# Layer 0 of a sparse graph-attention stack runs inside the load stage, a step for each loaded tile

## The reference

```python
def _L0_gnn_ref(inputs, adj, W, a):
    Wh = inputs @ W
    e = (Wh @ a[:F_out, 0])[:, None] + (Wh @ a[F_out:, 0])[None, :]
    e = jnp.where(e > 0, e, ALPHA * e)
    scores = jnp.where(adj > 0, e, NEG_BIG)
    attention = jax.nn.softmax(scores, axis=1)
    return jax.nn.elu(attention @ Wh)
...
x = _layernorm(x + _L0_gnn_ref(x, adj, L0_gnn_W, L0_gnn_a), axis=-1)
x = _layernorm(x + _L1_gnn_ref(...), axis=-1)   # slope 0.01, a bias, no elu
x = _layernorm(x + _L2_gnn_ref(...), axis=-1)   # as layer 0
x = _layernorm(x + _L3_gnn_ref(...), axis=-1)   # slope 0.01, elu
```

## Time and profile before

| | us |
|---|---|
| median of 3 runs | 621.22 (620.89 to 625.52) |
| the profiled execution, its own time | 624.31 |
| its span, first to last instruction | 622.4 |
| DVE, ACT, PE and POOL busy in the span | 408.7, 364.4, 361.5, 330.4 |
| indirect gathers on POOL | 340, 330.2 busy |
| adjacency transfers | 32 of 2048 KB |

### The profile page before, as it was taken

How to read it: one execution, slowest core, us unless ns; L and a number is a source line. 1 busy time by engine, 2 the same in 40 slices (tenths; PEclk the granted TensorE clock), 3 DMA queues, 4 the chain that set the end, 5 groups by cost and what they waited for, 6 DMA issues and landing times.

```text
span 622.4 us, 11074 instructions
## 1 busy us (share of the span) xinstructions
PE 361.5 (58%) x3546; PEld 322.1 (52%) x3558; DVE 408.7 (66%) x1830; ACT 364.4 (59%) x797; POOL 330.4 (53%) x344
## 2 busy tenths in 40 slices
PE   2365422323332589885278777527887752787663
PEld 1254311322222589784278667427877642786662
DVE  2897869799979628896235768623575862357576
ACT  3575775766674268883076667307666740676563
POOL 0000574156555700017777777767777777777760
PEclk9999999999999989996599989659988975999896
DMA  7998999999993200002222222222222222222220
GB/s 264 416 400 311 365 368 403 420 405 401 413 408 110 25 1 10 19 21 49 29 27 28 37 47 47 45 29 30 28 37 46 45 46 32 29 37 36 44 45 22
DMA packets 22084, 86.74 MB, mean 139 GB/s; under 512 B 6851, under 2 KB 12102, under 8 KB 17798
## 3 DMA queue, kind: packets, MB, share of 16 engines
q1 hardware_dynamic: 10102, 73.39, 29.4%
q0 software_dynamic: 10880, 11.51, 13.4%
q10 hardware_dynamic: 1040, 1.08, 0.5%
HBM read 80.58 MB, written 5.37 MB: 138 GB/s over the span
## 4 chain that ended last, share of the span: by engine, by line
POOL 32%; DMA 18%; DVE 15%; issue 13%; ACT 10%; PE 8%; POOLq 0%; ACTq 0%; DVEq 0%
POOL xg L392 32%; DMA arena<-in_adj_t 16%; ACT arena L679 6%; PE bank L590 3%; PE bank L564 2%; DVE key L1093 2%; DVE arena L1066 1%; DMA xg<-table,index 1%; DVE stats L1118 1%; ACT arena L705 1%; PE bank L453 1%; DVE found L868 1%; DMA table<-wh 1%; DVE mean_var L1121 1%; DVE key L1115 1%
## 5 line engine op out<-in xcount | busy, mean ns | idle before, releaser
L392 POOL DMA_INDIRECT xg<-table,index x340 | 330.2, 971 | 274.7 <-issue 98.7
L705 ACT ACTIVATE arena<-bank,sloped_own 128x256 f32<-128x256 f32 (+3 forms) x144 | 76.8, 536 | 142.3 <-PE bank L564 141.6
L1066 DVE CUSTOM_DVE_ANT_0 arena<-bank,arena 128x256 f32<-128x256 f32 (+3 forms) x144 | 71.3, 499 | 130.9 <-ACT arena L705 130.7
L679 ACT ACTIVATE arena<-arena,half 128x4096 bf16<-128x4096 int32 x32 | 118.6, 3708 | 48.3 <-DMA arena<-in_adj_t 46.2
L564 PE MATMUL bank<-packed,xg 128*128 128x128 f32 x744 | 117.8, 296 | 36.0 <-DMA xg<-table,index 34.5
L590 PE MATMUL bank<-xg,arena 128*128 128x64 f32 x744 | 105.4, 281 | 11.8 <-ACT arena L723 11.5
L564 PEld LDWEIGHTS bank<-packed,xg 128*128 128x128 f32 x744 | 111.1, 213 | 2.2
L590 PEld LDWEIGHTS bank<-xg,arena 128*128 128x128 f32 x744 | 98.9, 202 | 16.7 <-ACT arena L723 16.1
L714 ACT ACTIVATE arena<-arena,neg_max 128x256 f32<-128x256 f32 (+3 forms) x144 | 81.1, 564 | 1.2 <-DVE neg_max L1075 1.1
L577 PE MATMUL bank<-packed,arena 128*128 128x128 f32 x372 | 65.5, 283 | 10.1 <-ACT arena L723 8.2
L561 PE MATMUL bank<-off_row,wall 128*128 128x256 bf16 (+2 forms) x132 | 42.8, 325 | 45.1 <-DMA xg<-table,index 40.4
(11 more groups left out here) (128 smaller groups left out, 505.9 us busy)
## 6 DMA issues: line engine op xcount, KB each, us to landing
arena<-in_adj_t SPq DMA_DIRECT2D x32, 2048.0 KB, 12.2
xg<-table,index POOLq DMA_INDIRECT x340, 2.8
table<-wh SPq DMA_DIRECT2D x24, 132.0 KB, 1.7
table<-wh ACTq DMA_DIRECT2D x1, 1056.0 KB, 6.0
x<-in_x SPq DMA_DIRECT2D x1, 1024.0 KB, 10.7
out_x<-x SPq DMA_DIRECT2D x8, 128.0 KB, 2.1
slot_row<-in_c_slot_row SPq DMA_DIRECT2D x1, 384.0 KB, 11.2
packed<-in_c_packed SPq DMA_DIRECT2D x1, 352.0 KB
```

The lines of the kernel that those rows point to most:

```text
L392: pool.indirect_dma_start(out=xg[:, c, :], out_offset=None, in_=table[l][0:rows, :], in_offset=bass.IndirectOffsetOnAxis(ap=index[:, c:c + ...
L679: nc.scalar.activation(masks[:, t % 2, :], arena[:, t % 3, :], ACT.Sign, bias=half[:, :]).then_inc(mask_made, 1)
L705: nc.scalar.activation(score[:, n % RING, 0:m * P], score_ps[n % len(score_ps)][:, 0:m * P], ACT.Relu, bias=sloped_own[:, k:k + 1], scale= ...
L1066: nc.vector.tensor_tensor_reduce(out=y, in0=score_ps[n % len(score_ps)][:, 0:m * P], in1=y, scale=1.0, scalar=MASKED, op0=ALU.add, op1=ALU ...
```

## The change

Layer 0's rounds move into the load stage: from turn 10 on each turn also runs one round of layer 0, on every engine, and what is left of the rounds (there are 49, since a round of layer 0 now handles one segment and not one tile, and the stages behind the masking lag by two rounds more) runs after the last turn, before the flag is read. Layers 1 to 3 keep their rounds. With it go:

- The tiles come in the order 0, 20 to 31, 1 to 19 (`BATCHES`), and layer 0 takes them in the order 20 to 31, 0, 1 to 19 (`ORDER`), so that its groups end in the order 5, 6, 7, 0, 1, 2, 3, 4.
- `list_neighbours` is split: the words in the batch's last turn (`TOP_AT`), the marks one turn later, the columns two, the picking three turns later. Tile 0's columns are split over turns 2, 3 and 4, and it is picked in turn 8.
- Layer 0 has buffers of its own (`score_0` with 6 slots, `slots_0` with 4), since the arena's slots hold the adjacency. The former aliases of `key` and of the arena become buffers; the product of the lonely rows with the mean row, 2048 wide at the start of a layer, is now made for each group in `combine` (`lone`, 256 wide).
- PSUM is dealt anew: 2 banks for codes instead of 3, one bank (`room_ps`) for all of the lists and offsets, one accumulator bank for layer 0, one bank for the turned scores of layer 0 until segment 24.
- POOL gathers a batch's chunks as soon as its index is there, without a wait for codes between them.
- The next layer's rows are turned no earlier than round 25 of layer 0.

The diff, cut to its core; `slope` to `own`, `spread`, `turn` and `aggregate` keep their instructions but for the numbers of their semaphores and the lines shown:

```diff
-BATCHES = [(0, 1), (20, 4), (24, 4), (1, 3), (4, 4), (8, 4), (12, 4), (16, 4), (28, 2), (30, 2)]
+BATCHES = [(0, 1), (20, 4), (24, 4), (28, 4), (1, 3), (4, 4), (8, 4), (12, 4), (16, 2), (18, 2)]
 TURN0 = [sum(n for _, n in BATCHES[:b]) for b in range(len(BATCHES) + 1)]
 TILE_AT = [k for k0, n in BATCHES for k in range(k0, k0 + n)]
 TURN_OF = [TILE_AT.index(k) for k in range(TILES)]
-CHUNK_AT = [c for k0, n in BATCHES for c in range(FIRST[k0], FIRST[k0 + n])]
-CHUNK0 = [sum(FIRST[k0 + n] - FIRST[k0] for k0, n in BATCHES[:b]) for b in range(len(BATCHES) + 1)]
...
-CODE_BANKS = 3
-GATHER_START = 2
-GATHER_SHARE = 3
+CODE_BANKS = 2
...
+RING0 = 6
+TRING0 = 4
+
+
+ORDER = [list(range(20, TILES)) + list(range(0, 20))] + [list(range(TILES))] * (LAYERS - 1)
+TILE_POS = [[order.index(k) for k in range(TILES)] for order in ORDER]
+GROUP_ORDER = [[order[GROUP * p] // GROUP for p in range(GROUPS)] for order in ORDER]
+GROUP_POS = [[order.index(g) for g in range(GROUPS)] for order in GROUP_ORDER]
+SEG_POS = [[sum(SEGN[j] for j in order[:order.index(SEGS[q][0])]) + q - SEG0[SEGS[q][0]] for q in range(NSEG)]
+           for order in ORDER]
+
+
...
+STEPS = [[[q] for k in ORDER[0] for q in range(SEG0[k], SEG0[k] + SEGN[k])]] + [
+    [list(range(SEG0[k], SEG0[k] + SEGN[k])) for k in order] for order in ORDER[1:]]
...
+WAIT_SEGS = max(SEGN) - 1
+LAG = [{stage: lag + (WAIT_SEGS if l == 0 and stage not in ("spread", "slope", "mask") else 0)
+        for stage, lag in LAG_TILE.items()} for l in range(LAYERS)]
+ROUNDS = [len(STEPS[l]) + max(LAG[l].values()) for l in range(LAYERS)]
+FIRST_TURN = 25
...
+TURN_X_AT = [[max(GROUP_STEP[l][p] + LAG[l]["turn_x"], FIRST_TURN + p if l == 0 else 0) for p in range(GROUPS)]
+             for l in range(LAYERS)]
...
+LATE = 24
+
+
+def turned_bank(n):
+
+    return n % 2 if n >= LATE else 0
...
+LAST = [TURN0[b + 1] - 1 for b in range(len(BATCHES))]
+BEATS = LAST[-1] + 4
+TOP_AT = [[b for b in range(len(BATCHES)) if LAST[b] == t] for t in range(BEATS)]
+MARK_AT = [[b for b in range(len(BATCHES)) if LAST[b] + 1 == t] for t in range(BEATS)]
+CAND_AT = [[b for b in range(1, len(BATCHES)) if LAST[b] + 2 == t] for t in range(BEATS)]
+WIDE_AT = {2: 0, 3: 1, 4: 2}
+PICK_AT = [[b for b in range(len(BATCHES)) if (LAST[b] + 3 if b else 8) == t] for t in range(BEATS)]
+PICK_ORDER = [b for t in range(BEATS) for b in PICK_AT[t]]
+ROUND_START = 10
+OVER_ROUND = 30
+SLOPE_BEAT = 7
+
+
+def rounds_at(t):
+
+    return [t - ROUND_START] if t >= ROUND_START else []
 
 
...
+        codes_ps = [banks[0], banks[1]]
+        room_ps = banks[2]
+        score_ps = [banks[3], banks[4]]
+        turned_ps = [banks[5], banks[0]]
+        agg_ps = [banks[6], banks[2]]
+        first_xt_ps, next_xt_ps = banks[5], banks[1]
+        wh_ps = banks[7]
...
+            for g in GROUP_ORDER[0]:
+                write_rows(0, g)
...
-            def gather_some(count, made):
...
+            pool.wait_ge(written, 16)
+            for i, b in enumerate(PICK_ORDER):
+                k0, n = BATCHES[b]
+                pool.wait_ge(index_made, i + 1)
+                for c in range(FIRST[k0], FIRST[k0 + n]):
...
+                if turned_bank(n) == 1:
+                    pe.wait_ge(codes_read, TILES)
+                if turned_before(n) >= 1:
+                    pe.wait_ge(turned_copied, turned_before(n))
...
+                agg = agg_ps[ng % 2 if l >= 1 else 0]
+                if k % GROUP == 0 and c0 == 0 and ng >= 1:
+                    pe.wait_ge(agg_read, ng - 1 if ng >= GROUPS + 2 else ng)
...
+            done_rounds = 0
+            for t in range(BEATS):
+                if t < TILES:
+                    pack(t)
+                    if 1 <= t <= GROUPS // 2:
+                        project_rows(2 * t - 2, 0)
+                        project_rows(2 * t - 1, 0)
+                    if t == 0:
+                        pe.wait_ge(x_loaded, 16)
+                    if t < GROUPS // 2:
+                        turn_rows(2 * t, 2 * t, xt_copied, 2 * t)
+                        turn_rows(2 * t + 1, 2 * t + 1, xt_copied, 2 * t)
+                for b in PICK_AT[t]:
+                    lists(b)
+                if t == SLOPE_BEAT + 1:
+                    sum_rows(0)
+                for i in rounds_at(t):
+                    run_round(0, i)
+                    done_rounds = i + 1
+                for b in TOP_AT[t]:
                     first_slots(b)
-                if b >= 1:
-                    lists(b - 1)
-            pe.wait_ge(over_made, 1)
-            nc.tensor.matmul(off_ps[:, 0:1], ones[:, :], over_sum[:, :], start=True, stop=True).then_inc(over_summed, 1)
-
-            sum_rows(0)
+            for i in range(done_rounds, ROUNDS[0]):
+                run_round(0, i)
+                if i == OVER_ROUND:
...
+                link(nc.vector.tensor_tensor(lone[:, h, :, :], sum_wh[:, :].unsqueeze(1).broadcast_to([P, GROUP, F]),
+                                             lonely[:, k0:k0 + GROUP].unsqueeze(2).broadcast_to([P, GROUP, F]), ALU.mult))
...
+            for t in range(BEATS):
+                for i in rounds_at(t):
+                    run_round(0, i)
+                    done_rounds = i + 1
+                if t < TILES:
+                    first_round(t)
+                for b in MARK_AT[t]:
+                    mark_slots(b)
+                for b in PICK_AT[t]:
+                    pick_neighbours(b)
+                for b in CAND_AT[t]:
+                    list_columns(b)
+                if t in WIDE_AT:
+                    wide_part(0, WIDE_AT[t])
+                for b in TOP_AT[t]:
+                    list_words(b)
+                if t == SLOPE_BEAT:
+                    v.wait_ge(wh_copied, GROUPS)
+                    for g in range(GROUPS):
+                        slope(0, g)
+                    sum_columns(0)
+                if t == SLOPE_BEAT + 2:
+                    start_layer(0)
+
             link(nc.vector.tensor_tensor(over[:, 0, :], deg[:, :], limits[:, 0, :], ALU.is_gt))
             link(nc.vector.tensor_tensor(over[:, 1, :], from_end[:, :], limits[:, 1, :], ALU.is_gt))
...
```

821 lines of the change are left out of this document (424 added, 397 removed).

## The result

The changed kernel takes 636.55 us (median of 4 runs, 635.82 to 637.97), the kernel before 621.44 us (4 runs, 620.89 to 625.52): a ratio of 1.0209 with a 95% interval of 1.0163 to 1.0256. It is 15 us slower. The profiled execution has a span of 635.9 us, 13.5 more than the 622.4 of before; both profiled executions lie 1.4 to 2.9 us above the median of their kernel.

What follows compares the result with a forecast made beforehand. It took the time as T, when layer 1's table has landed, plus a part layer 0 cannot shorten. Terms: -13.4 (T) + 17.5 (gathers) + 1.3 (lone product) = +5.4 us on 621.2, so 627 us; range 609 to 645.

Steps and rivals of the forecast that it cites:

- the likeliest case: Whole kernel: the forecast itself holds, 617 to 637 us; chance 0.45.
- part 4: Layer 1: the 14 early gathers wait for the last group, so all 85 stand behind T; +17.5 us.
- part 1: Load stage: DVE sets the pace, 110.3 us for 16 turns plus 3 us of waits; turn 31 at 224 us.
- rival C: Load stage: ACT and DVE work in lockstep, and PE's spread waits for masking with two score banks; 645 us, chance 0.24.
- part 2: End of the load stage: 17 us from turn 31 until the last batch is picked, at 241 us.
- part 3: Rest of layer 0: 18.4 us of spreads, 4.8 for single-bank waits, 19 to T; T at 283 us.
- T: Landing of the last piece of layer 1's table: 296.4 us before, forecast at 283 us, 13 us earlier.
- The lone product: Tails of layers 1 to 3: each group's own 256-wide product adds 0.42 us per layer, +1.3 us.
- A: Load stage: the DMA keeps the pace and the added work falls into DVE's waits; 601 us, chance 0.08.
- B: Load stage: half of A's gain, PE's single-bank waits vanish, turn 31 at 214 us; 612 us, chance 0.2.
- D: Layer 1: the 14 gathers' extra wait does not appear, as low groups' writes end early; 610 us, chance 0.03.
- The rule that was weighed: PE in the load stage: full clock assumed; throttled by default would cost some 1.9 us more for each of 25 rounds.

Runs made afterwards that it cites:

- experiment 1: The kernel before, with layer 1's 14 early gathers also waiting for the whole table: 642.02 us against 623.96 for the kernel before on that chip.
- experiment 5: The changed kernel, with ELU exponential and centering one round later, root and scaling two later, for the three groups ending in the load stage: 638.83 us.
- experiment 6: Masking one round earlier in the load stage: 637.56 us on the changed kernel, 620.41 us on the kernel of experiment 2.
- experiment 2: The changed kernel with tile order 0, 20 to 23, 1 to 19, 24 to 31 and tile 0's pick one turn earlier: 615.82 us.
- experiment 3: The kernel of experiment 2, with layer 1's 14 early gathers behind the whole table: 627.89 us, against 624.04 for the kernel before.
- experiment 4: The changed kernel with no round of layer 0 in the load stage, all 49 following it: 648.21 us.
- experiment 7: The changed kernel with tiles in natural order 0 to 31, tile 0's wide lists in turns 1 and 2 and its pick in turn 3: 617.55 us.

## Why the prediction was right, and where it was not

Forecast 627 us with 609 to 645; measured 636.6, slower as the larger chance said, at the upper edge of the likeliest case (617 to 637) and within the range. The range is 36 us wide and held outcomes of both signs; the forecast change was +5.4 us and the measured one is +15.1, so what was right is the account of what pays and what gains, and not its size. By its steps:

- **The gathers (part 4), +17.5 us.** Right: 16.8 between the profiles, 17.1 and 18 in experiment 1. (The text calls a group's piece of the table a quarter megabyte; it is 132 KB, and nothing hangs on it.) This term decides the sign of the result, and it came from asking who reads the table first, not from layer 0 at all.
- **DVE's load stage (part 1).** Turn 15 at 111 us: 112.0. Work for 16 turns 110.3 us: the stretch less its waits for codes is 118.4 - 7.0 = 111.4. The mis-sized term is the waits on the other engines: I put 3 us, and 7.0 came, so turn 31 stands at 230.4, not 224. I counted only whether each engine's mean turn fits below DVE's 6.9 us, and in means they do. Experiments 5 and 6 show that the waits do not belong to one alone of the two queues that I blamed in rival C: undoing either leaves the stretch at 116 to 119 us. What sets the 7.0 us stays open.
- **The end of the load stage (part 2), 17 us.** 15.6 (230.4 to 246.0).
- **The rest of layer 0 (part 3).** From the last index to tile 9's spread 1.6 us pass (247.60 - 245.98), where I had none. The spreads of tile 9 to 19 take 270.67 - 247.60 = 23.1 us, predicted 18.4 + 4.8 = 23.2. The single accumulator bank was the part of it without a row, and PE's waits for DVE's combine (L655 for `num`) sum to 4.5 us in 4 waits behind 240 us. From the last spread to T: 21.0 us for 19. The 2 us are not explained; the granted clock averaged 0.64 there, as it did over the same piece of the kernel before (279.34 to 296.40 us).
- **T** is thus 291.7 instead of 283: 1.0 (turn 15) + 5.4 (the stretch: 4.0 of waits, 1.1 of work, rounding) - 1.4 + 1.6 + 2.0 make 8.6 of the 8.7 us. The gathers took 0.7 us less than forecast and the lone product 0.1 more: 8.1 us of miss between the profiles. The rest of the miss in the total (627 to 636.6) is that the medians differ by 15.1 us and the two profiled spans by 13.5.
- **The lone product, 1.3 us**: layers 2 and 3 took 1.3 + 0.1 us more. The sum agrees by luck: 0.42 us was forecast for each of the layers 1 to 3, but layer 2 has 1.3, layer 3 has 0.1, and layer 1 took less than the gathers alone would make it. Layer 2 took 108.4 and 108.3 us in the two kernels without the lone product (before, experiment 1) and 109.0 to 109.8 in the others of experiments 2 to 7; that it is this product no run shows.
- **What was to be seen** came in part: 85 gathers in a row behind T, masks that hardly wait for the DMA (1.4 us in two waits), DVE busy for 0.89 of the stretch (over 0.9 was said), layers 2 and 3 unchanged within 1.3 us (1 was said). Turn 31 near 224 and the last write near 283 did not: 230.4 and 291.7. Rivals A and B (the DMA keeps the pace, wholly or half) fail on the mask pace of (230.4 - 112.0) / 16 = 7.4 us; D on the gathers.
- **Rival C** had the sign and a mechanism that exists (ACT waits 11.0 us for DVE's centering in the trace), but at 18 us it was dear: removing that part gave at most 2.5 us back in the stretch and nothing in the time. Its other part, the score banks, was removed by itself too (experiment 6); the two were never removed together.
- **What I did not see** is that the new tile order leaves DVE idle for 17 of the 60 us from 50 to 110. I wrote that the added work fits there; that the same turns could take work off the full ones was the larger point, worth 9 to 11 us (experiment 3).

**The rule that was weighed.** I costed PE's rounds in the load stage at the full clock, by the rows. The clock did fall, to between 0.50 (the 1.2 GHz level) and 0.62 from 180 to 230 us in this profile, with PE busy 6.2 to 8.3 us in 10 (6.9 on average). In the 60 us before (110 to 170) it had been 1.00 with PE busy 3.9 to 7.4 us in 10 (5.7 on average), in the kernel before it was 1.00 at 2.2 to 2.9, and from 250 to 270 us of this profile it was 1.00 again, with PE busy 8.6 to 9.3 us in 10. By the Trainium skill ("TensorE: Matmul & The Clock Gate", What's actually happening) the throttled state is the default and activity releases it. The return at 250 us agrees with that, the fall in a stretch that was busier than the one before it does not, and the full clock with PE mostly idle is not what I had read out of it either; no rule comes out of these rows. Without rounds in the load stage (experiment 4) the clock stayed at 1.00 up to 280 us. For the time it mattered little, as far as runs show: experiments 5 and 6 ran the stretch at 0.96 and 1.00 and took 115.9 and 118.6 us for it, against 118.4 at 0.80, though each had an edit besides; and of the four executions of experiment 5 the fastest (635.18 us) had the lowest mean clock (0.844, the others 0.857 to 0.883).
